# Cross-attention on one core: the first query chunk multiplied as plain float32 from the load ring

## What is computed

```python
memory_proj = jnp.einsum('bme,de->bmd', memory, W_mem)
scores = jnp.einsum('bnd,bmd->bnm', hidden_states, memory_proj) / jnp.sqrt(jnp.float32(D))
attn = jax.nn.softmax(scores, axis=-1)
memory_context = jnp.einsum('bnm,bmd->bnd', attn, memory_proj)
gate_input = jnp.concatenate([hidden_states, memory_context], axis=-1)
gate = jax.nn.sigmoid(jnp.einsum('bnf,df->bnd', gate_input, W_gate) + b_gate)
fused = hidden_states + gate * memory_context
return _rmsnorm(fused, norm_w)
```

## Time and profile before

| | |
|---|---|
| median of 3 runs | 120.50 us (120.46 to 120.71) |
| the profiled execution, own time | 120.74 us |
| its span, first to last instruction | 119.0 us |
| TensorE busy | 112.3 us, 94% of the span |
| VectorE, ScalarE, GpSimd busy | 76.7, 55.1, 19.5 us |
| mean granted clock of TensorE | 0.987 of full speed |
| transfers | 18.45 MB, 155 GB/s over the span |

### The profile page before, as it was taken

How to read it: one execution, slowest core, us unless ns; L and a number is a source line. 1 busy time by engine, 2 the same in 40 slices (tenths; PEclk the granted TensorE clock), 3 DMA queues, 4 the chain that set the end, 5 groups by cost and what they waited for, 6 DMA issues and landing times.

```text
span 119.0 us, 1570 instructions
## 1 busy us (share of the span) xinstructions
PE 112.3 (94%) x547; PEld 94.2 (79%) x547; DVE 76.7 (64%) x116; ACT 55.1 (46%) x100; POOL 19.5 (16%) x25
## 2 busy tenths in 40 slices
PE   6999999999999999999999999999999999999910
PEld 6878888888888888888888888888888888889900
DVE  0389969987999700459999857464662031777791
ACT  4498675559967930941624532512421030334511
POOL 2000000000000499692000300030301000011120
PEclk9999999999999999999999999999999999999995
DMA  3999992436955870000436495749222200044222
GB/s 54 338 343 357 390 389 77 150 111 187 265 198 167 248 258 10 0 0 0 176 116 237 116 323 158 293 116 241 83 88 102 80 0 0 0 123 141 88 88 88
DMA packets 11095, 18.45 MB, mean 155 GB/s; under 512 B 1232, under 2 KB 4048, under 8 KB 11088
## 3 DMA queue, kind: packets, MB, share of 16 engines
q1 hardware_dynamic: 10656, 17.70, 45.2%
q10 hardware_dynamic: 432, 0.66, 1.8%
HBM read 14.16 MB, written 4.19 MB: 154 GB/s over the span
## 4 chain that ended last, share of the span: by engine, by line
PE 85%; issue 4%; DVE 4%; ACT 2%; POOL 1%; POOLq 1%; DVEq 0%; ACTq 0%
PE wide L716 18%; PE acc L767 18%; PE wide L785 16%; PE acc L691 10%; PE wide L813 6%; PE wide L798 6%; PE wide L744 5%; PE wide L676 3%; PE wide L730 3%; ACT squares L394 2%; DVE gate L546 2%; DVE gate L539 2%; POOL rstd L323 1%; POOLq L29 1%; ACT res L457 0%
## 5 line engine op out<-in xcount | busy, mean ns | idle before, releaser
L323 POOL TENSOR_TENSOR rstd<-mean_sq,neg_half 128x1 f32<-128x1 f32 x8 | 5.9, 734 | 55.7 <-ACT squares L394 52.6
L358 ACT ACTIVATE probs<-wide,neg_max 128x1024 f32<-128x1024 f32 x8 | 8.9, 1116 | 8.4 <-DVE neg_max L482 8.4
L716 PE MATMUL wide<-ctxT_hi,qT_hi 128*128 128x512 f32 x32 | 12.6, 392 | 0.0
L716 PE MATMUL wide<-ctxT_hi,qT_lo 128*128 128x512 f32 x32 | 12.5, 389 | 0.0
L716 PE MATMUL wide<-ctxT_lo,qT_hi 128*128 128x512 f32 x32 | 12.5, 389 | 0.0
L318 POOL TENSOR_TENSOR wgT_lo<-ring,wgT_hi 128x512 fp32r<-128x512 f32 x4 | 5.4, 1373 | 38.9 <-ACT wgT_hi L344 38.9
L523 DVE TENSOR_TENSOR wgT_lo<-acc,wgT_hi 128x512 fp32r<-128x512 f32 x4 | 2.6, 686 | 13.6 <-ACT wgT_hi L383 13.6
L482 DVE TENSOR_REDUCE neg_max<-wide 128x1 f32<-128x1024 f32 x8 | 9.7, 1215 | 2.2 <-PE wide L716 2.1
L387 ACT ACTIVATE gate<-gate 128x512 f32<-128x512 f32 x7 | 4.4, 629 | 13.2 <-DVE gate L533 13.2
L785 PE MATMUL wide<-wgT_hi,xT_lo 128*128 128x512 f32 (+1 forms) x36 | 8.8, 365 | 0.0
L785 PE MATMUL wide<-wgT_lo,xT_hi 128*128 128x512 f32 (+1 forms) x36 | 8.8, 365 | 0.0
(11 more groups left out here) (91 smaller groups left out, 250.9 us busy)
## 6 DMA issues: line engine op xcount, KB each, us to landing
ring<-ctxT SPq DMA_DIRECT2D x8, 256.0 KB, 4.1
ring<-w_gateT SPq DMA_DIRECT2D x8, 256.0 KB, 5.5
ring<-ctxN SPq DMA_DIRECT2D x8, 256.0 KB, 5.4
xr<-x_rows SPq DMA_DIRECT2D x8, 256.0 KB, 3.3
passage<-ring SPq DMA_DIRECT2D x4, 512.0 KB, 3.6
ring<-passage SPq DMA_DIRECT2D x16, 128.0 KB, 2.8
out<-res SPq DMA_DIRECT2D x7, 256.0 KB, 2.0
ring<-xT SPq DMA_DIRECT2D x6, 256.0 KB, 5.5
```

Of the source, the lines that this page charges most:

```text
L323: nc.gpsimd.tensor_tensor(rstd[:, col], mean_sq[:, col], neg_half[:], ALU.pow)\
L358: nc.scalar.activation(probs[:, j % PROBS].rearrange("p (h m) -> p h m", h=2), wide[:, banks("scores", j)], ACT.Exp, bias=neg_max[:, j:j + 1],
L716: last = nc.tensor.matmul(wide[:, banks("scores", j), h], qT_s[left][:, c, rows], ctxT_s[right][:, c, cols], start=(c == 0 and (left, righ ...
```

## The change

- TensorE computes chunk 0 of the first sequence's queries in four matmuls of plain float32, straight from the ring: the raw w_mem block by the raw x block, slice after slice (`plain_queries`). Each waits for the two landed blocks and counts up a new semaphore, `plain_read`. Chunk 1 follows as a whole from the split tensors, 12 matmuls, with the order of the two mixed products swapped.
- The blocks are ordered anew: w_mem (0,0), x 0, x 1, w_mem (0,1), x 2, x 3, then w_mem (1,0) and (1,1). They were w_mem (0,0), x 0, w_mem (1,0), x 1, w_mem (0,1), x 2, w_mem (1,1), x 3.
- SP, before it refills a slot that held one of the x blocks or a w_mem block of chunk 0, waits for `plain_read` too.
- ACT's and DVE's steps for chunk 0's query move from behind block 9 to behind block 7. All blocks are still split.
- One warm-up matmul fewer, 34.

```diff
@@ constants
-    WARM = 35
+    WARM = 34
@@ the order of the blocks
         wm_block(0, 0)
         xT_block(0, 0)
-        wm_block(1, 0)
         xT_block(0, 1)
         wm_block(0, 1)
         xT_block(0, 2)
+        xT_block(0, 3)
+        wm_block(1, 0)
         wm_block(1, 1)
-        xT_block(0, 3)
@@
+        PLAIN_READS = {index_of["xT", 0, k]: k + 1 for k in range(KD)}
+        PLAIN_READS |= {index_of["wm", 0, h]: (h + 1) * KD // 2 for h in range(2)}
@@ SP
                     wait_hi(sp, i - RING)
                     wait_lo(sp, i - RING)
+                    if i - RING in PLAIN_READS:
+                        sp.wait_ge(plain_read, PLAIN_READS[i - RING])
                 sp.dma_start(slot(i), src).then_inc(loaded[i], 16)
@@ ACT
             def query_hi(b, c):
-                act.wait_ge(q_sum, nth_chunk(b, c))
+                if b == 0 and c == 0:
+                    act.wait_ge(plain_read, KD)
+                else:
+                    act.wait_ge(q_sum, KE * b + c)
@@
-            split_hi(0, 1, 2, 3, 4, 5, 6, 7, 8, 9)
+            split_hi(0, 1, 2, 3, 4, 5, 6, 7)
             query_hi(0, 0)
-            split_hi(10)
+            split_hi(8, 9, 10)
             query_hi(0, 1)
@@ DVE
-            split_lo(0, 1, 2, 3, 4, 5, 6, 7, 8, 9)
+            split_lo(0, 1, 2, 3, 4, 5, 6, 7)
             query_lo(0, 0)
-            split_lo(10)
+            split_lo(8, 9, 10)
             query_lo(0, 1)
@@ TensorE
+            def plain_queries(k):
+
+                wm_i, xT_i = index_of["wm", 0, 2 * k // KD], index_of["xT", 0, k]
+                pe.wait_ge(loaded[wm_i], 16)
+                pe.wait_ge(loaded[xT_i], 16)
+                last = nc.tensor.matmul(acc[:, 0], slot(wm_i)[:, k % (KD // 2)], slot(xT_i), start=(k == 0),
+                                        stop=(k == KD - 1))
+                last.then_inc(plain_read, 1)
...
-                    for left, right in ((HI, HI), (LO, HI), (HI, LO)):
+                    for left, right in ((HI, HI), (HI, LO), (LO, HI)):
@@
-            for k in range(KD // 2):
-                for c in range(KE):
-                    queries(0, c, (k,))
-            for c in range(KE):
-                queries(0, c, range(KD // 2, KD))
+            for k in range(KD):
+                plain_queries(k)
+            queries(0, 1)
```

More of the change, by code:

```diff
@@ L170, in xattn_kernel @@
         landed = [sem(f"landed{n}") for n in range(2)]
+        plain_read = sem("plain_read")
         q_hi, q_lo = sem("q_hi"), sem("q_lo")
@@ L676, in keep_warm, with queries @@
                     nc.tensor.matmul(wide[:, PAIRS - 1, 1, 0:P], warm[:], warm[:], start=True, stop=True)
-            def queries(b, c, ks):
-                if b and ks[0] == 0:
+            def plain_queries(k):
[5 more added lines that the diff above has]
+                last.then_inc(plain_read, 1)
+            def queries(b, c):
+                if b:
                     pe.wait_ge(q_lo, nth_chunk(b - 1, c))
-                for k in ks:
+                for k in range(KD):
                     wm_i, xT_i = index_of["wm", c, 2 * k // KD], index_of["xT", b, k]
-                    for left, right in ((HI, HI), (LO, HI), (HI, LO)):
+                    for left, right in ((HI, HI), (HI, LO), (LO, HI)):
                         if (left, right) == (HI, HI):
@@ L692, in queries @@
                                                 start=(k == 0 and (left, right) == (HI, HI)),
-                                                stop=(k == KD - 1 and (left, right) == (HI, LO)))
-                if ks[-1] == KD - 1:
-                    last.then_inc(q_sum, 1)
+                                                stop=(k == KD - 1 and (left, right) == (LO, HI)))
+                last.then_inc(q_sum, 1)
             def scores(j):
@@ L828, in _ @@
             scores(2)
-            queries(1, 0, range(KD))
+            queries(1, 0)
             turn(0)
@@ L832, in _ @@
             turn(1)
-            queries(1, 1, range(KD))
+            queries(1, 1)
             turn(2)
```

## The result

The changed kernel takes 121.45 us against 120.7 us, medians of nine runs each: 1.0058 of the time before, 95% interval 1.0035 to 1.0081. The profiled execution has 121.45 us and a span of 119.7 us; that of before had 120.74 and 119.0. The forecast was 121.1, slower by 0.63 us; it came 0.70 slower by the ratio and the spans. Of the 0.35 us between 121.1 and 121.45, 0.2 lie in the base: the kernel before has 120.7 in nine runs where three had given 120.50.

What follows compares the result with a forecast made beforehand. TensorE was taken as the bound: four float32 products of 3.52 us replace 2.72 us of split ones, scores start at 12.00 instead of 11.37, so 120.5 + 0.63 = 121.13, rounded 121.1 us; range 120.3 to 121.9.

Steps and rivals of the forecast that it cites:

- Price: Chunk 0 in the head: each of the four float32 products takes 0.88 us at the upper level, 3.52 us together.
- Slowdown at the lower level: TensorE in the head: work at the lower clock level goes 1.89 times as slowly as at the upper.
- The wait of 0.13 us that was to go: Head, first product: 0.13 us of waiting for the first low part of x, which the change would remove.
- step 3: The sum for the head: chunk 0 ends at 9.28, scores start at 12.00 instead of 11.37, 0.63 us later.
- the crosswise sum: Check on the head's loss: products 0.80 us more, less 0.13 of wait and 0.07 of earlier start, 0.60 us.
- The step to the upper level: TensorE in the head: its clock goes from 1.2 to 2.4 GHz at 6.72 us.
- The feed: Head: raw blocks and split parts arrive before TensorE wants them, no wait; the cover for chunk 1's weights is 0.6 us.
- The ring: SP's refill of slot 0 goes out at about 7.5 us, takes 3.5 and lands at 11.0: no stall.
- rival B: Scores of tile 0, second chunk: the ring refills too late, 5.1 us to landing, 0.2 to 0.8 us on top; chance 0.15.
- A: The four float32 products are cheap, 0.44 us each as the transposes: 119.5 us; faster 0.11, no change 0.13.
- C: The four products: weight loads of the float32 passes don't overlap, 1.66 us each, 3.1 us on top, 124.2; chance 0.05.
- D: The change does less than it says: splits of w_mem and x aren't saved; already in the forecast, not priced again.

Runs made afterwards that it cites:

- e4: The changed kernel with each float32 product made twice, first into a bank nobody reads: 124.28 us, ratio 1.0301, two runs.
- e9: The changed kernel once more, unaltered, for a second trace: 121.87 us, ratio 1.0069; its profiled execution took 123.37 us.
- e5: The changed kernel without the fourth float32 product, so slice 3 of the contraction is missing from chunk 0: 121.46 us, ratio 1.005.
- e8: The changed kernel without the fourth float32 product and with the blocks in the load order of before: 121.31 us, ratio 1.0011.
- e10: The kernel before with only slice 0 of chunk 0 as a float32 product, 35 warm-up matmuls kept: 120.89 us, ratio 1.0015.
- e11: The changed kernel with 40 warm-up matmuls instead of 34: 121.43 us, ratio 1.0069, six runs.
- e3: The kernel before with only slice 0 of chunk 0 as a float32 product and 30 warm-up matmuls instead of 35: 120.58 us, ratio 0.9958.
- e12: e3 once more, unaltered (one float32 product, 30 warm-up matmuls, against the kernel before): 120.69 us, ratio 1.0003.
- e7: The changed kernel with chunk 0 multiplied whole from the split tensors and the blocks in the load order of before: 122.99 us, ratio 1.0191.
- e1: The changed kernel with chunk 0 multiplied from the split tensors again (12 matmuls instead of 4 float32 ones), new load order kept: 123.06 us, ratio 1.0157.

## Why the prediction was right, step by step

**The direction and its cause**: right. TensorE's work in the head sets the time, a float32 product costs more than the three it replaces, and nothing gives it back.

**The sum**, term by term, against scores at 12.00 forecast and 12.12 found:

- Start: forecast 4.90, found 4.82; 0.04 us of work gained.
- Price: 0.88 forecast, 0.86 found (0.858 in e4); four times the difference is 0.08 less.
- Slowdown at the lower level: 1.89 assumed, from the split products; the float32 ones have 0.85 against 0.43, 1.98. Over the 1.93 us that they spend there this is 0.05 more.
- The wait of 0.13 us that was to go (step 3, and the head's 0.56 us in the first part): this step failed. The first recorded matmul of the changed kernel loses as much, by the starts (the first at 4.82):

```profile
5.81 1.56 PE L693 MATMUL acc<-ring 128*128 128x512 f32 x2
...
6.66 1.14 PE L693 MATMUL acc<-ring 128*128 128x512 f32 x2
```

Each row groups two matmuls and begins with the start of the first. 5.81 - 4.82 = 0.99 where the next takes 6.66 - 5.81 = 0.85, and no operand is waited for. It belongs to the first product behind the warm-up in both kernels, most likely its weight load, which has no matmul to lie beside (an inference, not tested). In the kernel before I had put it down to x's low part, although that part's product came only 0.43 us behind its predecessor. The 0.14 us are lost at the lower level and worth half, so plus 0.07; the crosswise sum, which takes off the whole 0.13, has it too large for the same reason.
- The step to the upper level: 6.72 assumed, 6.89 found by the record (and by the spacing: 6.67 to 7.21 is 0.54 us, which holds some 0.2 at the lower level). Plus 0.08.
- Chunk 1's 12 products: 2.72 forecast, 2.76 by the chain. Plus 0.04.

12.00 - 0.04 - 0.08 + 0.05 + 0.07 + 0.08 + 0.04 = 12.12, as found. That the forecast of 12.00 came so close is partly luck, since 0.12 us too much and 0.24 too little offset each other. The term that makes the loss, 3.44 us of float32 against 2.72 of split products, is 0.72, as large as the loss itself.

**The feed**: right in sizes. The transfers and the split of chunk 1's first weights in the changed kernel:

```profile
4.71 0.63 ACT L351 ACTIVATE xT_hi<-ring 128x512 fp32r<-128x512 f32 x1 [0.42 <-DMA ring<-xT]
5.96 0.63 ACT L351 ACTIVATE xT_hi<-ring 128x512 fp32r<-128x512 f32 x1 [0.62 <-DMA ring<-xT]
```
```profile
8.77 0.75 DVE L482 TENSOR_TENSOR wm_lo<-ring,wm_hi 128x256 fp32r<-128x256 f32 x2
```

The second x block is there at 5.96 (5.9 forecast), the low part of those weights at about 8.77 + 0.42 = 9.19 (9.13 forecast). The first x block came at 4.71, not 4.26: the start at 4.82 has 0.1 us to spare, not 0.6, and that is where e9 and e4 start late. That a landing can be 0.6 to 1.1 us later in another execution wasn't in the range of any term.

**The ring**: the first refill went out at 7.9 instead of 7.5 and landed 3.0 us later (3.5 forecast), at 10.9; the second landed 4.2 us after 8.3. No stall in the first trace of the changed kernel, as the sum had it. But rival B is real: block 11 came at 13.2 to 13.8 in e5, e8, e10 and e11, and from the scores' start to the next queries these take 0.3 to 1.0 us more than the 8.32 of the kernels before and changed. It took 0.15 of the chances as an alternative to the forecast; it is rather an event of single executions, for e3 and e12, which differ from e10 only in having fewer warm-up matmuls, don't show it. Its place was named one block too early: block 10 never held up TensorE, block 11, which is issued behind it, did.

**The rivals**: A and C are refuted by e4. D's remark holds, all splits are still made. Not tested by themselves are the swapped order of the mixed products and the earlier steps of ACT and DVE; the sum above leaves nothing for them.

**The level of the clock**: its rise was treated as a place in time, the same for both kernels. The traces show that it moves from execution to execution, and that behind a gap of 0.6 us or more ahead of the first product it can come 3 us later, which costs 1.5 to 1.6 us of time (e9, e7, e1). That is more than the whole change.

## What to carry to other kernels

Count the passes of a matmul's type before trading splits for raw operands: here 4 against 3 lost 0.7 us, since TensorE is the bound, and relief for other engines is worth nothing as long as they aren't late. When one bound is lowered, price the next two before counting the gain: here 0.86 us of products taken away brought nothing that could be measured, because a split and a refilled ring slot stood a few tenths behind. Let the warm-up run into the landing, with a margin for late landings, rather than end before it: six small matmuls too many cost nothing that was measured, and fourteen too few went with 1.3 us more in the median of two runs.

## What was not expected of the hardware

- A float32 matmul of 128x512 is recorded as two matmuls with a weight load each, 0.43 us apart at the upper level and 0.85 at the lower; the loads lie beside the matmuls and add nothing.
- The column of the granted clock reads 1.00 in the head of all fourteen traces, while the same product goes every 0.43 us and later every 0.23. The record behind it begins with the rise, and its first entry agrees with the spacing in every trace: 6.89 us in the changed kernel, 10.33 in e1, whose distances fall from 0.43 to 0.40 and 0.23 between 9.98 and 10.61. Ahead of the first entry the column says nothing.
- TensorE's step to the upper level came anywhere from 5.10 to 10.33 us after the span's start, from 5.44 to 10.33 with the same 34 warm-up matmuls. The Trainium skill, TensorE: Matmul & The Clock Gate, Part 1, says that the throttled clock is the default and that activity releases it; the traces agree in that every late step follows idle time of 0.6 us or more.
- The first x block, always issued at 0.8 us as one of the first two transfers, was taken up by ACT between 4.3 and 5.4 us in the fourteen traces.
